# A vision tower with product-key experts: own banks and a third set of banks in the dense stage, and the last token tile's top-k placed among the final rounds

## The reference

```python
q = (hidden @ w_queries.T).reshape(b, t, 2, h, n)          # h = 4 heads, n = 32
sim = einsum('btphn,hkpn->pbthk', q, keys)                 # 128 keys a head, p = 0, 1
sx, ix = top_k(sim[0], 8)
sy, iy = top_k(sim[1], 8)
all_scores = sx[..., :, None] + sy[..., None, :]           # 64 pairs a head
scores, pos = top_k(all_scores, 8)                         # the best 8 pairs
indices = take(ix * 128 + iy, pos)                         # of 4096 experts
ew = silu(einsum('btd,bthkd->bthk', hidden, down_embed[indices])) * softmax(scores)
experts_states = einsum('bthk,bthkd->btd', ew, up_embed[indices])
mlp = silu(hidden @ w_gate.T) * (hidden @ w_up.T) @ w_down.T
return h + mlp + experts_states
```

## Time and profile before

| | us |
|---|---|
| median of the three runs | 276.38 |
| the three runs | 276.38, 274.52, 276.57 |
| the profiled execution | 274.73 |
| its span | 272.9 |
| TensorE busy | 244.9 |
| VectorE busy | 179.7 |

### The profile page before, as it was taken

The page is one execution under the profiler, slowest core; times in us unless marked ns, Lnnn a source line. Parts: engine busy times, 40 slices in busy tenths (PEclk is TensorE's granted clock), DMA queues, the critical chain, the costliest instruction groups (busy, mean ns, idle before and its releaser), DMA issues.

```text
span 272.9 us, 4832 instructions
## 1 busy us (share of the span) xinstructions
PE 244.9 (90%) x1956; PEld 203.2 (74%) x1956; DVE 179.7 (66%) x455; ACT 56.9 (21%) x104; POOL 54.8 (20%) x71
## 2 busy tenths in 40 slices
PE   3998975798855999899999899899979999999996
PEld 2675645687632588889898899888868888888763
DVE  0056297878886049999999999799968767511100
ACT  1101135353371241323132734100000000000000
POOL 5024055124222523325042520000000000000000
PEclk9999999999985699999999999999999999999999
DMA  7970000220003351061125520200000000000000
GB/s 251 387 236 0 2 0 1 95 71 30 17 20 97 97 174 42 18 207 47 40 67 166 149 83 1 91 0 2 0 19 2 0 19 2 0 19 2 19 0 12
DMA packets 14805, 16.99 MB, mean 62 GB/s; under 512 B 848, under 2 KB 12992, under 8 KB 14784
## 3 DMA queue, kind: packets, MB, share of 16 engines
q1 hardware_dynamic: 13776, 15.70, 17.8%
q10 hardware_dynamic: 1008, 1.00, 1.1%
HBM read 15.48 MB, written 1.21 MB: 61 GB/s over the span
## 4 chain that ended last, share of the span: by engine, by line
PE 55%; DVE 37%; issue 3%; ACT 2%; DMA 1%; POOL 1%; DVEq 0%
PE ps L1063 23%; PE ps L1026 9%; PE ps L818 7%; PE ps L1085 5%; DVE topi L694 3%; DVE big L793 3%; PE ps L982 3%; DVE xn L513 3%; DVE top L691 3%; PE ps L1060 3%; DVE big L545 2%; PE ps L895 2%; PE ps L845 2%; DVE red L587 1%; DVE big L589 1%
## 5 line engine op out<-in xcount | busy, mean ns | idle before, releaser
L1063 PE MATMUL ps<-ue,big 128*128 128x256 f32 (+1 forms) x320 | 72.3, 381 | 1.4 <-DVE big L793 1.4
L1063 PEld LDWEIGHTS ps<-ue,big 128*128 128x128 f32 (+1 forms) x320 | 57.2, 182 | 12.1 <-DVE big L793 1.8
L1026 PE MATMUL ps<-hn_hi,de_hi 128*128 128x296 f32 x128 | 40.7, 318 | 2.1 <-ACT big L480 1.1
L793 DVE TENSOR_TENSOR big<-ps,big 128x1024 f32<-128x1024 f32 (+1 forms) x19 | 22.7, 1197 | 26.9 <-PE ps L1085 26.2
L1026 PE MATMUL ps<-hn_lo,de_hi 128*128 128x296 f32 x128 | 38.3, 300 | 0.0
L1026 PE MATMUL ps<-hn_hi,de_lo 128*128 128x296 f32 x128 | 38.2, 299 | 0.0
L480 ACT ACTIVATE big<-ps 128x592 f32<-128x592 f32 x32 | 21.1, 666 | 44.5 <-PE ps L1026 44.4
L1026 PEld LDWEIGHTS ps<-hn_hi,de_hi 128*128 128x128 f32 x128 | 24.1, 188 | 4.5 <-DVE actT L740 1.9
L1026 PEld LDWEIGHTS ps<-hn_lo,de_hi 128*128 128x128 f32 x128 | 24.1, 188 | 1.2 <-issue 1.2
L1026 PEld LDWEIGHTS ps<-hn_hi,de_lo 128*128 128x128 f32 x128 | 24.1, 188 | 0.0
L679 DVE TENSOR_TENSOR late<-eqx,wsel 128x2048 f16<-128x2048 f16 (+1 forms) x19 | 22.7, 1197 | 0.7
(11 more groups left out here) (113 smaller groups left out, 335.5 us busy)
## 6 DMA issues: line engine op xcount, KB each, us to landing
de<-in_down_t SPq DMA_DIRECT2D x16, 256.0 KB, 2.8
ue<-in_up_e SPq DMA_DIRECT2D x4, 1024.0 KB, 5.6
big<-in_patches SPq DMA_DIRECT2D x6, 296.0 KB, 5.1
big<-in_w_tok ACTq DMA_DIRECT2D x6, 128.0 KB, 5.5
big<-in_w_qkv SPq DMA_DIRECT2D x1, 768.0 KB, 8.4
h_scratch<-big SPq DMA_DIRECT2D x5, 111.0 KB
late<-in_keys_bd SPq DMA_DIRECT2D x1, 512.0 KB, 9.6
downT<-in_wdown_t SPq DMA_DIRECT2D x1, 512.0 KB, 9.2
```

The costliest lines, as they stand in the source:

```text
L793: chain(nc.vector.tensor_tensor(dst, pv, dst, ALU.mult), g_ready)
L1026: last = mm(ps[:, 2 + 2 * (e % 2) + a, 0:HALF], half[:, (e // 2) % SPLITS, k, own], src[:, k, a * HALF:(a + 1) * HALF], start=(n == 0), st ...
L1063: last = mm(acc, sil[:, e, j * 128:j * 128 + Q * v], ue[:, e, :], start=False, stop=(e == EX - 1))
```

## The change

- The keys are laid out in pairs of heads (`keys_pairs`, 128 by 256 for each `p`). The sims of a tile are four matmuls, each of 64 partitions (two heads) with 256 columns; heads 0 and 1 go to bank 6, heads 2 and 3 to bank 7. They wait for both key searches of the tile before and count `pe_sim` once.
- The up product goes to banks 0 and 1. It waits for the gated product before it. `sg` has two buffers. The first two blocks of a segment no longer wait for the gated product; block 18, the first in banks 0 and 1, waits for all four.
- From block 16 on the blocks go round three sets of banks, (2, 4, 0), and from block 19 on a block waits for the silu of block `e - 3`.
- VectorE's top-k of tile 4 leaves the dense stage. The differences and the exponential are taken for tiles 0 to 3 at once, the exponential ahead of the silu of block 25 instead of 21, then their weights. Tile 4's parts follow the products of rounds 4, 5, 7 and 9, its weights that of round 10; its exponential is behind all silus.
- Round 0 waits for the silu of block 30 and round 1 for that of block 31, because of the banks.

```diff
+GATED = 16
+EXP_AT = 25
...
-        sg = slots[:, 6 * D:6 * D + T]
+        sg = (slots[:, 6 * D:6 * D + T], rows[:, 0:T])
...
+        def dense_bank(e):
+
+            return 2 + 2 * (e % 2) if e < GATED else (2, 4, 0)[(e - GATED) % 3]
...
+            sp.wait_ge(gu_done, IC)
             for j in range(TILES):
                 r = Q * valid(j)
                 sp.dma_start(resid[0:r, j, :], h_dram[j * 128:j * 128 + r, :]).then_inc(ld_res, 16)
...
-                    if j == TILES - 1 and i == 5:
-
-                        act.wait_ge(lg_ready, TILES)
-                        nc.scalar.activation(ex[:, :, :, :], ex[:, :, :, :], ACT.Exp).then_inc(lg_exp, 1)
+                    if e == EXP_AT:
+
+                        act.wait_ge(lg_ready, 1)
+                        nc.scalar.activation(ex[:, 0:IC], ex[:, 0:IC], ACT.Exp).then_inc(lg_exp, 1)
                     act.wait_ge(pe_s, e + 1)
...
                 if j < IC:
                     act.wait_ge(pe_gate, j + 1)
-                    if j >= 1:
-                        act.wait_ge(gu_done, j)
+                    if j >= 2:
+                        act.wait_ge(gu_done, j - 1)
...
+            act.wait_ge(lg_ready, 2)
+            nc.scalar.activation(ex[:, IC:TILES], ex[:, IC:TILES], ACT.Exp).then_inc(lg_exp, 1)
...
+            for j in range(IC):
+                best_keys(j, 0)
+                best_keys(j, 1)
+                best_pairs(j)
+                if j == IC - 1:
+                    logits(0, IC)
+                places(j)
+                gated_product(j)
+            weights(0, IC, 1)
             for i in range(RING):
                 build_slots(i)
...
                 elif RING <= i < len(rounds) - RING:
                     build_slots(i + RING)
+                if i == 4:
+                    best_keys(IC, 0)
+                elif i == 5:
+                    best_keys(IC, 1)
+                elif i == 7:
+                    best_pairs(IC)
+                    logits(IC, TILES)
+                elif i == 9:
+                    places(IC)
+                elif i == 10:
+                    weights(IC, TILES, 2)
                 if t0 + w == valid(j) and j >= 1:
                     finish(j - 1)
...
-            def sims(j, p):
+            def sims(j):
                 if j >= 1:
-                    pe.wait_ge(sim_read, 2 * (j - 1) + p + 1)
-                mm(ps[:, 6 + p, :], qT[:, p, j * 128:(j + 1) * 128],
-                   keysBD[:, p, :, :].rearrange("p h k -> p (h k)"), start=True, stop=True).then_inc(pe_sim, 1)
+                    pe.wait_ge(sim_read, 2 * j)
+                for p in range(2):
+                    for i in range(2):
+                        own = slice(2 * FN * i, 2 * FN * (i + 1))
+                        last = mm(ps[:, 6 + i, p * 2 * NK:(p + 1) * 2 * NK],
+                                  qT[own, p, j * 128:(j + 1) * 128], keys2[own, p, :], start=True, stop=True)
+                last.then_inc(pe_sim, 1)
...
-                    if j >= 1 and i < 2:
-
-                        pe.wait_ge((gate_act, gu_done)[i], j)
+                    if j >= 1 and i == 0:
+
+                        pe.wait_ge(gate_act, j)
+                    if e == GATED + 2:
+
+                        pe.wait_ge(gu_done, IC)
...
-                        pe.wait_ge(sil_ready, e - 1)
+                        pe.wait_ge(sil_ready, e - 1 if e < GATED + 3 else e - 2)
...
-                    pe.wait_ge(sil_ready, e)
-                    gated(4, (up_hi, up_lo), j, pe_gu)
+                    if j >= 1:
+                        pe.wait_ge(gu_done, j)
+                    gated(0, (up_hi, up_lo), j, pe_gu)
...
-                    if n_p == 1:
-                        pe.wait_ge(sil_ready, EX - 1)
+                    if n_p < 2:
+                        pe.wait_ge(sil_ready, EX - 1 + n_p)
```

More of the change, by code:

```diff
@@ L683, in build_slots, with best_keys, best_pairs @@
                     .broadcast_to([128, c, 2 * Q, EX, 2]), ALU.mult), slots_ready)
[L685 to L695, removed]
+            def best_keys(j, p):
+                dve.wait_ge(pe_sim, j + 1)
+                simv = ps[:, 6:8, p * 2 * NK:(p + 1) * 2 * NK].rearrange("p a (h k) -> p a h k", h=2)
+                behind()
+                for hh in range(FH):
+                    chain(nc.vector.max(top[:, p, hh, :], simv[:, hh // 2, hh % 2]))
+                behind()
+                for hh in range(FH):
+                    chain(nc.vector.max_index(topi[:, p, hh, :], top[:, p, hh, :], simv[:, hh // 2, hh % 2]),
+                          sim_read if hh == FH - 1 else dve_chain)
+            def best_pairs(j):
                 behind()
@@ L703, in _, with places @@
                 for hh in range(FH):
-                    chain(nc.vector.max(best[:, hh, :], cf[:, hh, :]))
+                    chain(nc.vector.max(best[:, j, hh, :], cf[:, hh, :]))
                 behind()
                 for hh in range(FH):
-                    chain(nc.vector.max_index(besti[:, hh, :], best[:, hh, :], cf[:, hh, :]))
-                chain(nc.vector.tensor_tensor(ex[:, j], best[:, :, :],
-                                              best[:, :, 0:1].broadcast_to([128, FH, TOPK]), ALU.subtract), lg_ready)
+                    chain(nc.vector.max_index(besti[:, hh, :], best[:, j, hh, :], cf[:, hh, :]))
+            def places(j):
                 behind()
@@ L745, in _ @@
[L745 to L754, removed]
@@ L764, in _, with gated_product @@
-            for j in range(TILES):
-                for a in range(2):
-                    chain(nc.vector.tensor_tensor(wsel[:, j, :, a], own,
-                                                  by_pairs(packT[:, j, 2 + a, :]).unsqueeze(2)
-                                                  .broadcast_to([128, TT // 2, Q, 2]), ALU.mult))
+            def gated_product(j):
+                dve.wait_ge(gate_act, j + 1)
+                dve.wait_ge(pe_gu, j + 1)
+                chain(nc.vector.scalar_tensor_tensor(halves(actT[:, j, :]), halves(sg[j % 2]), WSCALE,
+                                                     ps[:, 0:2, 0:HALF], ALU.mult, ALU.mult), gu_done)
@@ L1025, in _ @@
                         for n, (half, src, k) in enumerate(parts):
-                            last = mm(ps[:, 2 + 2 * (e % 2) + a, 0:HALF], half[:, (e // 2) % SPLITS, k, own],
+                            last = mm(ps[:, dense_bank(e) + a, 0:HALF], half[:, (e // 2) % SPLITS, k, own],
                                       src[:, k, a * HALF:(a + 1) * HALF], start=(n == 0), stop=(n == len(parts) - 1))
@@ L1029, in _ @@
                     if e == 1:
-                        sims(0, 0)
-                        sims(0, 1)
+                        sims(0)
                     e += 1
```

70 lines of the change are left out of this document (43 added, 27 removed).

## The result

The changed kernel takes 286.85 us (median of four runs, 286.57 to 288.12) against 276.48 before (four runs): ratio 1.041, 95% interval 1.038 to 1.045. The profiled execution has a span of 284.9 us, against 272.9. So the medians differ by 10.4 us and the profiled executions by 12.0: that of the kernel before, 274.73 us, is 1.8 us under its median, that of the changed kernel, 286.97, is near its own. What follows accounts for the two profiled executions.

A forecast was written before the change was run, and what follows sets the result against it. VectorE was taken to set the end in two stretches, TensorE in the others. Terms -0.1 + 4.3 + 3.4 = +7.6, taken as +7.5, on the median 276.38 gave 283.9 us; range 279.5 to 289.

The forecast's parts named there:

- the likeliest case: VectorE's longer order sets the end, with G between 143.3 and 148.6: +4.9 to +10.3 us; chance 0.66.
- rival (c): TensorE's clock falls in its new waits after round 1 and before round 7's product ends: 287 to 289; chance 0.19.
- three signs of being wrong: VectorE idle before round 7's product; TensorE waiting under 3 us together before tile 1's and 2's experts; clock not 1.00.
- G: End of the gated product of tile 3, 145.86 us before; forecast 145.9, with ends 143.3 and 148.6.
- Block 18 and TensorE's early start: Block 18 starts at G, where block 17 did; TensorE ready for round 0 at G + 23.0, 3.1 us early.
- the hit stays: VectorE loses 0.76 us a tile to GpSimd at L709; with the subtraction gone, a later operation is hit instead.
- The exponential: At block 25, VectorE waits for it until G + 14.0; 14 us idle replace 12 of top-k, net +1.9.
- Key search before X: Tile 4's key search after rounds 4 and 5 adds 4.33 before X, end of round 7's product: 203.7, +4.2.
- Tile 2: From X, end of round 7's product, to tile 2's experts: VectorE's added pieces make it 23.1 against 19.7, +3.4.
- (a): TensorE's chain decides, top-k hides in VectorE's idle time and the 3.1 us early start counts: 273.3; chance 0.07.
- (b): The halves balance: G at 143.3 or earlier, weights and places shorter, stalls partly absorbed: 276 to 279; chance 0.08.
- (d): The row groups don't overlap: sims cost 1.7 us as before; no change of the sum, part of the forecast.

The follow-up runs named there:

- e7: Kernel before the change, with only the keys laid out in pairs of heads: 277.12 us, ratio 1.006.
- e10: Kernel before the change, with the subtraction of tiles 0 to 3 moved behind the gated product: 275.65 us, ratio 1.000; start of first key search (K) to G 46.21.
- e3: Changed kernel with tile 4's top-k, except its weights, back behind the last gated product and the exponential at block 18: 276.86 us, ratio 1.003.
- e1: Changed kernel with the exponential of tiles 0 to 3 ahead of the silu of block 18 instead of 25: 284.72 us, ratio 1.030.
- e4: Changed kernel with 34 and 23 unused matmuls in TensorE's waits ahead of the experts of tiles 1 and 2: 284.48 us, ratio 1.030.
- e11: Changed kernel with tile 4's top-k spread over VectorE's idle time, round 10's slot build later, third banks from block 18, exponential at block 16: 269.21 us, ratio 0.978.
- e5: Changed kernel, exponential at block 18, tile 4's key search, pairs, logits behind the last gated product, places behind product 7, weights behind product 11: 272.66 us, ratio 0.988.
- e2: Changed kernel with tile 4's top-k, except its weights, back behind the last gated product, exponential still at block 25: 276.62 us, ratio 1.002.

## Why the prediction was right, and where it was not

The measured 286.85 us lies in the range, on the side forecast, but 3 us above the forecast: the median rose by 10.4 us, not by 7.5. The kernel is slower for the reason given, VectorE's longer order, and also for one that the likeliest case put at nothing. That case had TensorE's clock at 1.00 through its waits. It fell to 0.50 at three of them, as rival (c) had it, on top of the order and not instead of it: of the 12.05 us between the profiled executions, 7.6 stay when two of the waits are filled (forecast 7.5) and 4.4 go (rival (c): 3 to 5). Of the prediction's own three signs of being wrong two appeared, the clock, and VectorE idle ahead of the product of round 7: 0.72 us, ahead of that of round 3. The chance of 0.19 for (c) was low, seen from here: the rows had no wait that long at full clock, and so left the question open.

The agreement of 7.6 with 7.5 is partly luck. G came 1.0 us earlier than forecast, and the missed 1.0 was made up by 0.4 us of clock between D and X and by 0.6 in the experts' stretches.

**Keys in pairs.** 1.1 us a tile instead of 0.9, and no gain in time, as said (e7, which is even 0.6% slower).

**Block 18 and TensorE's early start.** Block 18 started at G, after a wait of 1.5 us, not 3.2: the sims of tile 4 began at 138.75, G - 6.1, when tile 3's key search had been over since 137.40, so TensorE had not caught up as far as forecast. TensorE was at round 0 at 167.94, G + 23.1 (forecast G + 23.0), and waited 3.3 us there behind round 1. Its gain ended as a wait.

**G.** Forecast 145.9, measured 144.83. The hits of 0.76 us in tiles 1 to 3 are gone: with TensorE's new pace GpSimd's operations fall mostly on key searches, which keep their time, and tiles 1 and 2 take 11.10 us instead of 11.86. Tile 0 has one of 1 us instead (1.27 at L709 in the chain above, 0.54 before), and in tile 3 the last operation ahead of the gated product takes 0.61 us instead of 0.19, beside GpSimd's cast (143.49 to 144.10): tile 3 is as long as before, to 0.1. The step that failed is "the hit stays": that an operation behind L709 is as exposed as it was is true (e10), but whether GpSimd runs at that moment is a matter of phase. The skill's rule (the Trainium skill, SBUF — State Buffer, "SBUF: two separate sides") says who waits for whom and for how long, and the five operations shown from e3, e7 and e10 end with GpSimd's, as it has it; for the casts and shifts among them, which have one input, that takes a two-port mode, which no trace shows. Whether they meet it can't say.

**The exponential.** VectorE idle 14.14 us, forecast 14.0; G to D 27.10, forecast 27.1. With G's 1.0 the first product came at 171.93 instead of 173.0. Seen from e1, the idle time costs 3.4 us, less than its 14, since TensorE allows no first product before G + 24.3. The weights of four tiles took 4.1 us, forecast 4.3.

**Key search before X.** D to X 31.34, forecast 30.68. The 0.66 more is the clock again, which fell behind the 3.3 us wait behind round 1: round 3 took 1.86 us instead of 1.08 and VectorE idled 0.72 us for it. In e1, without that wait, the stretch is 30.72.

**Tile 2.** X to the experts of tile 2 26.09, forecast 23.1. With the clock kept up (e4) it is 23.46, so the step was right to 0.4 and the rest is round 8 coming late, as rival (c) had it. The prediction set the fall near 80 us beside the rule that a wait between bursts lets the clock fall; that is loose, since TensorE's waits between 70 and 82 us are 0.4 to 2.2 us long there, and a wait of 2.5 us in e7 had no fall behind it. Tile 3's 1.7 us are nearly all clock (e4: 19.52).

**Rivals (a), (b), (d).** (a) fails at its own condition: D at G + 27.1, and the key search ahead of X without idle time. e11 comes near it, with D at G + 22.5 and 6.3 us less than before. (b) needed 5 us to vanish; 1.0 did, at G. (d) is out: the sims take 1.1 us, not 1.7.

**What stays open.** Why the clock ahead of K differs from one execution to the next, and whether the 1.7 us between 12.05 and 10.4 lie there: only the profiled executions have a trace. Whether the exponential at 25 was of any use: no run here shows one. And two gaps of VectorE that no wait in the traces explains: 0.35 us ahead of the second slot build behind D in e5, and the same ahead of D in e2 and e3.

## What to carry to other kernels

An engine at 66% can be the one that sets the end. Work taken off its chain in one stage and put into a later one is a gain only if the later place has idle time ahead of the point for which the other engine waits: with the exponential at block 18 in both, the same 12 us of top-k and weights cost 12.3 us more, clock included, behind rounds 4 to 10 (e1) than spread over VectorE's idle time (e5). If an engine's work is moved away from in front of a wait, look up when that wait is over; here the exponential stood where the top-k's end had been, and the time freed turned into idle time. A new wait of TensorE can have a second price behind it, in the clock: those of 3.3, 4.8 and 3.7 us had here, 4.8 us in all.

## What the runs showed of the hardware

- After 4.8 us of waiting TensorE resumed at 0.50 of its clock (1.2 GHz), and sixteen f32 matmul records took 6.35 us instead of 3.72; matmuls whose results nobody uses, in the wait, kept it at 1.00 (e4). Behind K the thirteen traces have nine TensorE waits of 3.2 to 5.8 us, each with a fall to 0.50 in it or right behind it, and no fall at any other wait (the longest is 2.5 us, in e7).
- Matmuls of 64 partitions in two row groups, f32, 256 columns: a tile's eight records in 1.09 us, where the full-height ones of 512 columns took 0.87 us for half a tile: 1.6 times as fast, not twice.
- A VectorE cast, shift or two-input operation that started inside one of GpSimd's lasted until its end: 0.20 us became 1.34, 0.18 became 1.16, 0.42 became 1.40 (e3). In the thirteen traces each of the 48 casts to `topf` that started beside a GpSimd operation took longer than the 0.20 us alone. Key searches reading PSUM kept their time beside GpSimd (MAX8 0.89 us for four, FIND_INDEX8 0.29), and so did the reductions (0.42).
